# Second pass of a graph attention layer: the exponentials of a group are turned back ahead of the step's message products

## What is computed

```python
e = (ea_f @ W_e).reshape(-1, H, C)                       # H = 4 heads of C = 32
s = leaky_relu(x_l[src_f] + x_r[dst_f] + e, 0.2)
alpha = einsum('ehc,hc->eh', s, att)
amax = segment_max(alpha, dst_f, num_segments=n)
ex = exp(alpha - amax[dst_f])
denom = segment_sum(ex, dst_f, num_segments=n)
out = segment_sum(x_l[src_f] * (ex / denom[dst_f])[:, :, None], dst_f, num_segments=n) + bias
```

## Time and profile before

| | us |
|---|---|
| median of 3 runs | 1480.98 (1479.98 to 1482.34) |
| the profiled execution, its own time | 1481.07 |
| its span, first to last instruction | 1479.0 |
| PE busy in the span | 1158.1 (78%) |
| DVE busy | 1017.9 (69%) |
| POOL busy | 951.6 (64%) |
| ACT busy | 835.1 (56%) |
| mean granted TensorE clock | 0.933 of full speed |

### The profile page before, as it was taken

One profiled execution on the slowest core, in us unless ns is written; L12 is line 12 of the kernel. 1 busy time (PEld: TensorE's weight loads), 2 busy tenths in 40 slices (PEclk: granted clock), 3 DMA queues, 4 the chain that ended last, 5 costly groups with the idle time before them and its releaser, 6 DMA issues. The chain is left out here.

```text
span 1479.0 us, 33421 instructions
## 1 busy us (share of the span) xinstructions
PE 1158.1 (78%) x8811; PEld 1040.1 (70%) x8811; DVE 1017.9 (69%) x2386; ACT 835.1 (56%) x2266; POOL 951.6 (64%) x947
## 2 busy tenths in 40 slices
PE   5876768878878878867897888887887888888860
PEld 3866757867877877856665787877777787777740
DVE  6342246656655675656646888888988888898866
ACT  4765535544544546627345865666666666666515
POOL 1777777776775767760007577777777777777504
PEclk9998879999999999989998999999999999999985
DMA  3433255544554545635111333333333333333101
GB/s 98 119 110 94 84 161 162 163 144 143 165 153 124 164 143 176 190 105 141 43 49 50 108 100 91 100 104 93 100 99 100 99 99 99 96 97 101 42 1 43
DMA packets 177449, 160.97 MB, mean 109 GB/s; under 512 B 23342, under 2 KB 145034, under 8 KB 177272
## 3 DMA queue, kind: packets, MB, share of 16 engines
q1 hardware_dynamic: 148088, 100.83, 23.7%
q0 software_dynamic: 29184, 58.01, 13.1%
HBM read 127.11 MB, written 34.39 MB: 109 GB/s over the span
## 5 line engine op out<-in xcount | busy, mean ns | idle before, releaser
L400 POOL DMA_INDIRECT sorted_rows<-row,place_idx x456 | 463.1, 1016 | 192.4 <-issue 167.2
L1259 POOL DMA_INDIRECT xl<-xl_rows,src_idx x436 | 445.7, 1022 | 149.0 <-issue 130.2
L485 ACT COPY row<-ps_x 125x512 f32<-125x512 f32 x114 | 66.7, 585 | 261.4 <-PE ps_x L877 235.0
L1538 PE MATMUL ps_cs<-w_e,attr_t 128*125 128x128 f32 x912 | 186.6, 288 | 0.6 <-issue 0.6
L1539 PE MATMUL ps_cs<-src_sum,onehot_ct 128*125 x912 | 185.9, 288 | 0.0
L680 DVE SCALAR_TENSOR_TENSOR onehot_s<-column,pair_bucket,row_in 128x128 f32<-128x128 f32 x488 | 138.6, 345 | 27.5 <-DMA row_in<-sorted_rows 16.0
L877 PE MATMUL ps_x<-x_nodes,onehot_t 128*125 x912 | 131.2, 290 | 29.4 <-issue 29.3
L1538 PEld LDWEIGHTS ps_cs<-w_e,attr_t 128*125 128x125 f32 x912 | 148.0, 203 | 0.8 <-issue 0.8
L877 PEld LDWEIGHTS ps_x<-x_nodes,onehot_t 128*125 128x125 f32 x912 | 117.2, 198 | 44.6 <-issue 44.3
L1272 ACT ACTIVATE apart<-column,dst_lo 125x128 f32<-125x128 f32 x456 | 145.4, 394 | 5.2 <-PEq L965 5.2
L1539 PEld LDWEIGHTS ps_cs<-src_sum,onehot_ct 128*125 128x125 f32 x912 | 147.1, 203 | 0.0
(11 more groups left out here) (333 smaller groups left out, 2305.6 us busy)
## 6 DMA issues: line engine op xcount, KB each, us to landing
row_in<-sorted_rows SPq DMA_DIRECT2D x135, 264.0 KB
attr<-in_ea SPq DMA_DIRECT2D x456, 62.5 KB
attr_c<-in_ea SPq DMA_DIRECT2D x456, 62.5 KB
sorted_rows<-row,place_idx POOLq DMA_INDIRECT x456
xl<-xl_rows,src_idx POOLq DMA_INDIRECT x456, 3.3
xl_rows<-x_nodes SPq DMA_DIRECT2D x5, 320.0 KB, 2.5
out<-x SPq DMA_DIRECT2D x4, 320.0 KB
sorted_rows<-x SPq DMA_DIRECT2D x5, 66.0 KB, 2.0
```

Source lines behind the costliest of these rows:

```text
L400: pool.indirect_dma_start(out=m.sorted_rows.rearrange("p k w -> (p k) w"), out_offset=bass.IndirectOffsetOnAxis(ap=m.place_idx[:, k:k + 1] ...
L1259: pool.indirect_dma_start(out=xl[off % RING][:, u, :], out_offset=None, in_=m.xl_rows, in_offset=bass.IndirectOffsetOnAxis(ap=m.src_idx[:, ...
L1538: pe.matmul(out, attr_t[off % 2][:, u, :], m.w_e[:], start=True, stop=False)
```

## The change

PE's turn back of the exponentials moves, within the same step b = 2, from behind the message products to ahead of them, together with its two waits (`exp_done`, `seam_ready`). It now stands right behind the transposes of the carries. The instructions are the same, and nothing else of the program changes.

```diff
                     mm.then_inc(carry_turned, 1)
+                if b == 2 and middle:
+                    pe.wait_ge(exp_done, grp)
+                    pe.transpose(ps_b[0:TE, 0:R], shifted[:], m.ident[0:R, 0:R])
+                    pe.transpose(ps_b[0:TE, R:2 * R], run[:, 0, :], m.ident[0:R, 0:R])
+                    pe.wait_ge(seam_ready, grp)
+                    pe.matmul(ps_b[:, 208:208 + 2 * H], seam_row[:], change8[:], start=True, stop=True).then_inc(
+                        turned_back, 1)
                 if 0 <= w < NB:
                     pe.wait_ge(added, i * RING + w + 1)
                     clear_window(pe, m, ps_m, W)
...
                     mm.then_inc(ends_turned, 1)
-                if b == 2 and middle:
-                    pe.wait_ge(exp_done, grp)
-                    pe.transpose(ps_b[0:TE, 0:R], shifted[:], m.ident[0:R, 0:R])
-                    pe.transpose(ps_b[0:TE, R:2 * R], run[:, 0, :], m.ident[0:R, 0:R])
-                    pe.wait_ge(seam_ready, grp)
-                    pe.matmul(ps_b[:, 208:208 + 2 * H], seam_row[:], change8[:], start=True, stop=True).then_inc(
-                        turned_back, 1)
```

## The result

| | before | after |
|---|---|---|
| median, us (20 runs each) | 1479.99 | 1483.91 |
| lowest to highest, us | 1468.24 to 1484.06 | 1478.74 to 1489.96 |
| ratio to before, 95% interval | | 1.0036 (1.0022 to 1.0050) |
| the profiled execution, us | 1481.07 | 1483.32 |
| its span, us | 1479.0 | 1481.3 |

The changed kernel is slower, by some 4 to 5 us. The forecast was 1496.7, so the sign came out as forecast and the size didn't: a third or less of the 15.6 us. In the changed kernel the turn back has the lines L1561, L1562 and L1564 (L1576, L1577 and L1579 before), the message products L1572 (L1565 before); the others keep theirs.

The account below looks back on a forecast made before the run. DVE, and what it waits for on PE, was taken to bound the second pass. Low-clock stretches, +19.7 us, less 4.1 for those gone at b = 5, gave +15.6 on 1481.07: 1496.7 us, range 1478 to 1508.

Parts of the forecast that it names:

- The turn back isn't earlier: PE, b = 2: the turn back can't start before ACT's exponential ends, so moving it wins 0 us.
- PE's two idles become one: PE, b = 2: its idles merge ahead of the turn back, 1.68 us in some groups, 2.95 us in others.
- One stretch at 1.2 GHz behind it: PE behind the turn back: on average one low-clock stretch per group, over products and b = 3 turns and scores; +19.7 us.
- the third rival: PE behind the turn back: two low-clock stretches in a row in each group, +37 us, 1518 us; chance 8%.
- The price of a stretch, 1.68 us: PE, turns and score products: 4.29 us with the low clock, 2.61 without, so 1.68 us of PE.
- The cover, 1.32 us: PE's idles at L133 in b = 3 and b = 4, 0.24 + 1.08 us, hide the move's 1.16 us, leaving 0.16.
- The factor 0.81: Share of PE's lateness reaching DVE at L1355: 1.36 of 1.68 us, giving 1.23 us for a group.
- DVE gets the moved products in time: DVE's L1463 of b = 3 started at 1105.93; the products would end about 1104.8, so the move alone costs 0.
- The low clock at b = 5 goes: PE ahead of b = 5: the gap shrinks to 1.12 us, so three low-clock stretches should go, -4.1 us.
- POOL isn't the pace: POOL's gathers wait for DVE's messages (8 times, 15.6 us), DVE never for a gather, so DVE sets the pace.
- L1355's idle of 2 us and more: DVE at L1355, waiting for scores turned by PE: idle expected at 2 us and more, 0.91 or more before.
- Rival two: PE behind the turn back: low clock in half the groups only, +5.7 us, 1486.8 us; chance 14%.

## Why the prediction came out as it did

- **The turn back isn't earlier: right.** L1561 starts 0.05 to 0.06 us behind the exponential's end in all of these groups, as before, and nothing was won.
- **PE's two idles become one: right.** 35.9 us in 16 times, 1.67 to 3.02 each.
- **One stretch at 1.2 GHz behind it: right for eleven of groups 2 to 17.** One kept the clock (group 11), and four had almost two stretches, the third rival's case, which I had given to all groups or none. All four of these stand behind gaps of 2.94 to 3.02 us, and none of the ten groups behind 1.67 to 1.72; but groups 6 and 8, behind 2.92 and 3.01, had one stretch, so the gap's length alone doesn't decide it. The rule of the Trainium skill that the prediction set against this ("TensorE: Matmul & The Clock Gate", section "Why this matters for your kernels") would have had the clock hold; the gaps of 1.68 us with a low clock behind them disagree.
- **The price of a stretch, 1.68 us: right.** L133 of b = 3 comes 6.14 us behind the turn back in the group shown, 4.48 with the gap filled: 1.66.
- **The cover, 1.32 us: this is the term that failed.** "From there to L1355 of the next group no such wait is left: PE's lateness after b = 4 arrives at DVE" is the step, and it is wrong. I added the idles at the two L133, took PE's lateness behind them as DVE's, and had called the 1.12 us ahead of L1500 in b = 5 register reading, but not asked whether it runs beside PE's lateness. It does. By starts the two clearings cover 1.78 (an idle counts from a modelled end, and so reads short), and the reads 0.82. Of 1.16 + 1.66 = 2.82 us, 2.6 are covered; 0.23 was left in the group shown, where the forecast had 1.52.
- **The factor 0.81: wrong and harmless.** What is beyond the cover is passed on whole (1.95 at L1500, 1.94 at L1355).
- **DVE gets the moved products in time: right at 2.4 GHz, wrong at 1.2.** I priced the low clock on PE's path alone. Where the products themselves run slowly, DVE waits for them, here in group 10 of the kernel after, in the timelines of PE and of DVE:

```profile
1135.08 0.35 PE L1561 MATMUL ps_back<-ident,shifted 96*125 96x96 f32 x1 [1.69 <-ACT shifted L1326]
...
1136.41 2.02 PE L1572 MATMUL ps_m<-message,onehot_c 125*128 125x136 f32 x8
...
1144.89 0.39 PE L133 MATMUL ps_m<-zeros 128*128 128x272 bf16 x2
```

```profile
1138.58 0.72 DVE L1463 TENSOR_TENSOR message_sum<-message_sum,ps_m 128x544 f32 x1 [0.43 <-PE ps_m L1572]
...
1158.07 0.29 DVE L1355 TENSOR_TENSOR bound<-score_rows 96x124 f32<-96x124 f32 x1 [1.10 <-ACT score_rows L1308]
```

  PE's L133 of b = 4 is no later here (9.81 us behind the turn back) than in the group without this wait (9.90), but L1355 is: 22.99 instead of 22.56. This lateness is DVE's own, and PE's cover doesn't hide it. Of the eleven groups with one low stretch seven have the wait, and L1355 comes 22.71 to 23.12 us behind the turn back; in the four without, 22.56 to 22.71. In the changed kernel with early reads it is the same: with a wait of 0.21 to 0.43 us 22.56 to 22.76, with 0.05 at most 22.22 to 22.40.
- **The low clock at b = 5 goes: right.** None is left; the three were worth 1.59 each over the mean of the other groups, 4.8 us in all, not 4.1. Against the eight groups that had the low stretch of b = 2 alone it is 1.43, close to the 1.36.
- **POOL isn't the pace: right.** It waits for DVE's messages twice as long (31.6 us instead of 15.6). **L1355's idle of 2 us and more: wrong**, at 0.96 to 1.74 us, by the cover above.

With the measured cover and factor the prediction's own sum would have been 16 x 0.23 - 4.8 = -1.1 us, no change. The four double stretches (5.4 us in all, against 0.9 for single ones) and what is left of the twelve other groups' 0.35 us over 0.23 (1.4 in all, by subtraction; DVE's new wait stands in seven of them) make it +4.8. So the errors partly offset each other: the cover was far too small, which made the forecast too high, and the double stretches and DVE's wait were left out, which made it too low. Rival two's 1486.8 lies nearest to the result, but by luck: it let half of the groups fall, and 15 of 16 did.

## What to carry to other kernels

Before pricing lateness, follow it from start to start down to the engine that sets the pace, and ask of every idle on the way, named "issue" too, whether it is time that passes anyway beside the lateness: such an idle is cover. Ask also who needs the work that will run slowly: here DVE waited for the moved products themselves. Bringing thin matmuls (few columns, as the turn back's) ahead of thick ones behind a wait can cost more than the wait, because the thick ones may then run at the low clock; matmuls of zeros in a gap, or register reads moved ahead of a wait, are cheap ways to find out what a gap costs. Then look what the next floor is before promising the gain: here DVE's own round ended some 0.1 us ahead of what PE's reads allowed.

## What the chip showed that I had not expected

- Gaps of 1.67 to 3.02 us with a thin turn back behind them (0.70 us at the full clock) were followed by 1.2 GHz in 15 of groups 2 to 17; with seven matmuls of zeros in the gap, the clock stayed at 1.00 behind the turn back in all of groups 2 to 18.
- Two reads of PE's registers, 0.85 us each, made the next matmul wait until 2.52 us after the clearing, though the products between took 1.16. With PE 4.5 us late, 0.37 us of idle was still left: the reads don't hide wholly behind queued matmuls.
- In the kernel with gaps filled and reads early the clock fell behind the turn back in ten of sixteen groups, in five of them for some 6.6 us, though 1.49 us of clearing and products stood between the last longer idle (2.11 us) and the turn back. All sixteen groups have that idle; what decides between them stays unexplained.
